# Second layer of late expert blocks: half of its row pieces as three float32r products, half as plain float32

## The reference, cut to what matters

```python
assign = jnp.argmax(x @ centroids.T, axis=1)            # one expert per token, 8 experts
xhat = (x - mu) * jax.lax.rsqrt(var + LN_EPS)           # D = 256
xn = xhat * ln_g[e] + ln_b[e]
h = relu(xn @ w1[e].T + b1[e])                          # F = 1024
y = x + h @ w2[e].T + b2[e]
out = a * y + (1 - a) * x                               # a = sigmoid(x @ centroids.T)[e]
```

## Time and profile before

| | us |
|---|---|
| median of 3 executions | 1070.82 (1069.94 to 1071.56) |
| the profiled execution, whole | 1071.78 |
| its span, first to last instruction | 1070.0 |
| PE busy in the span | 1056.2 (99%) |
| DVE / ACT / POOL busy | 798.6 / 670.3 / 495.2 |

### The profile page before, as it was taken

One profiled execution on the slowest core, in us unless ns is written; L12 is line 12 of the kernel. 1 busy time (PEld: TensorE's weight loads), 2 busy tenths in 40 slices (PEclk: granted clock), 3 DMA queues, 4 the chain that ended last, 5 costly groups with the idle time before them and its releaser, 6 DMA issues.

```text
span 1070.0 us, 24078 instructions
## 1 busy us (share of the span) xinstructions
PE 1056.2 (99%) x8454; PEld 945.2 (88%) x8454; DVE 798.6 (75%) x1907; ACT 670.3 (63%) x1820; POOL 495.2 (46%) x641
## 2 busy tenths in 40 slices
PE   8899999999999999999999999999999999999998
PEld 6789898989888888889898988888898999999997
DVE  7876888888888988888888988798886554444441
ACT  6765757575856767665757576676655646666551
POOL 2653554646464545555464646455454343222222
PEclk9999999999999999999999999999999999999999
DMA  6475676675857566767657585756467657766670
GB/s 208 99 185 135 168 188 165 168 188 141 218 137 200 150 180 157 192 165 189 169 154 196 145 219 137 199 140 156 95 162 222 250 179 267 233 225 228 226 259 30
DMA packets 159660, 190.51 MB, mean 178 GB/s; under 512 B 17453, under 2 KB 149037, under 8 KB 154672
## 3 DMA queue, kind: packets, MB, share of 16 engines
q1 hardware_dynamic: 155088, 179.09, 61.3%
q0 software_dynamic: 3360, 8.53, 2.2%
q10 hardware_dynamic: 1088, 1.31, 0.3%
HBM read 65.72 MB, written 46.07 MB: 104 GB/s over the span
## 4 chain that ended last, share of the span: by engine, by line
PE 94%; DVE 2%; POOL 1%; DMA 1%; ACT 1%; issue 1%; SPq 0%; POOLq 0%; ACTq 0%; DVEq 0%
PE psum L694 16%; PE psum L727 16%; PE psum L869 12%; PE psum L764 11%; PE psum L854 10%; PE psum L743 9%; PE psum L779 9%; PE psum L713 8%; PE psum L782 1%; POOL prob L1677 1%; DMA prob_t<-prob 1%; DVE neg_max L1291 0%; POOL w_o_lo L1731 0%; ACT prob L1037 0%; PE psum L794 0%
## 5 line engine op out<-in xcount | busy, mean ns | idle before, releaser
L1677 POOL TENSOR_TENSOR prob<-prob,inv_sum 128x512 f32<-128x512 f32 x176 | 182.8, 1053 | 203.0 <-DVE inv_sum L1297 202.3
L1037 ACT ACTIVATE prob<-psum,neg_max 128x256 f32<-128x256 f32 x352 | 164.5, 481 | 48.6 <-DVE neg_max L1291 39.6
L1291 DVE TENSOR_REDUCE neg_max<-psum 128x2 f32<-128x512 f32 x256 | 162.3, 673 | 36.5 <-PE psum L743 36.5
L869 PE MATMUL psum<-w,v_n 128*128 128x256 f32 x608 | 134.2, 379 | 0.0
L1303 DVE STREAM_TRANSPOSE prob<-prob 128x512 f32<-128x512 f32 x176 | 121.5, 699 | 9.3 <-POOL prob L1677 8.9
L869 PEld LDWEIGHTS psum<-w,v_n 128*128 128x128 f32 x608 | 114.2, 190 | 14.8
L1677 POOL TENSOR_TENSOR w_ring<-w_ring,inv_sum 128x512 f32<-128x512 f32 x76 | 78.2, 1042 | 78.4 <-DVE inv_sum L1297 78.0
L1044 ACT ACTIVATE head_out_hi<-psum 128x512 fp32r<-128x512 f32 x52 | 31.1, 598 | 114.3 <-PE psum L764 91.7
L1748 POOL DMA_INDIRECT out<-x_in,r_ring x38 | 39.8, 1048 | 127.0 <-DVE x_in L1535 126.7
L1027 ACT ACTIVATE v_n<-psum 128x512 f32<-128x512 f32 x128 | 78.3, 612 | 20.7 <-PE psum L727 20.7
L1016 ACT ACTIVATE k_hi<-psum 128x512 fp32r<-128x512 f32 x128 | 77.2, 604 | 18.1 <-PE psum L694 16.8
(11 more groups left out here) (185 smaller groups left out, 2712.6 us busy)
## 6 DMA issues: line engine op xcount, KB each, us to landing
sorted_rows<-filler SPq DMA_DIRECT2D x54, 660.0 KB, 5.0
prob_t<-prob SPq DMA_DIRECT2D x176, 128.0 KB, 2.8
w_ring<-prob SPq DMA_DIRECT2D x176, 128.0 KB
w<-in_experts SPq DMA_DIRECT2D x19, 1024.0 KB
w_ring<-in_experts SPq DMA_DIRECT2D x18, 1024.0 KB, 5.6
prob_t<-w_ring SPq DMA_DIRECT2D x76, 128.0 KB, 2.8
w_ring<-w_ring SPq DMA_DIRECT2D x76, 128.0 KB
w_ring<-normed SPq DMA_DIRECT2D x56, 128.0 KB, 3.0
```

The source lines that it names most:

```text
L869: last = pe.matmul(bank[:, 0:d_model], hid[:, s % 2, f, i * P:(i + 1) * P], w2[:, f * d_model:(f + 1) * d_model], start=(f == 0), stop=(f ...
L1037: act.activation(prob_at(u, bb)[:, :, parity, i], scores_i, ACT.Exp, bias=neg_max[:, at, i:i + 1], accum_out=prob_sum[:, at, i:i + 1]).the ...
L1291: dve.tensor_reduce(neg_max[:, (4 * u + n) % 8, :], psum[:, n, :].rearrange("p (i j) -> p i j", i=2), AXIS_X, ALU.max, negate=True).then_i ...
L1677: pool.tensor_tensor(probs, probs, inverse, ALU.mult).then_inc(s_soft, 1)
```

## The change

From block 4 on (`FIRST_SPLIT`) the second layer takes the hidden pieces 0 to 3 as high and low parts of type float32r, three products each, as the first layer does; pieces 4 to 7 stay plain. What is new per block:

- ACT (`relu_parts`): the first four activations go to a single raw buffer `hid_raw`, the last four to `hid_plain`; between the two, ACT waits for the second layer's weights and copies half of them, 128x1024, as the high part (`f_w2h`).
- DVE (`split_hidden`): for two pieces at a time a cast 128x512 to the high part and a subtraction 128x512 to the low part, behind `split_xn(s+2)` and ahead of `finish(s)`. `finish` writes its intermediate in `fin` and so waits for the buffer at its start.
- POOL (`low_weights_2`): one subtraction 128x1024 behind `add_base(s+2)` and ahead of `write_rows(s)`.
- TensorE (`layer_2_split`): waits for the four of them at its start, then 24 float32r and 8 plain matmuls.
- SP: the second-layer weights and b2 of block 5 are issued ahead of the wait for all scatters and for the late blocks' table, instead of behind the rows and first-layer weights of block 6.
- Memory: the parts lie over tensors that are dead by then (`v_n`, `prob`, `y_t`, `prob_t_even`, `head_out`, `w_o`).

```diff
+            w2_hl = [[w[:].rearrange(rule)[:, 0:FS * d_model].rearrange("p (f d) -> p f d", f=FS) for w in pair] for pair, rule in
+                     ((head_out, "p b c t -> p (b c t)"), (w_o, "p c n -> p (c n)"))]
@@ SP @@
+                load_weights_2(n_early - 1)
+                load_b2(n_early - 1)
                 scattered(n_batches)
                 run = block_steps(sp, count_empty(sp))
                 for s in range(n_early, n_slots + 1):
                     run(s, (load_vectors,), (load_rows,), (load_weights_1,))
-                    run(s - 1, (load_weights_2,), (load_b2,))
+                    if s > n_early:
+                        run(s - 1, (load_weights_2,), (load_b2,))
                     run(s, (move_rows,))
@@ PE @@
+                def layer_2_split(s):
+                    pe.wait_ge(f_w2h, s - FIRST_SPLIT + 1)
+                    pe.wait_ge(f_w2l, s - FIRST_SPLIT + 1)
+                    pe.wait_ge(f_hl, FS // 2 * (s - FIRST_SPLIT + 1))
+                    pe.wait_ge(f_ha, FC // 2 * s)
+                    def in_parts(bank, i, first):
+                        for n, (hw, hx) in enumerate(PASSES):
+                            for f in range(FS):
+                                last = pe.matmul(bank, hid_hl[hx][:, s % 2, f, i * P:(i + 1) * P], w2_hl[s % 2][hw][:, f, :],
+                                                 start=(first and n == 0 and f == 0), stop=(not first and n == 2 and f == FS - 1))
+                        return last
...
+                    bank = begin(("fy", s, 0))[:, 0:d_model]
+                    in_parts(bank, 0, True)
+                    plain(bank, 0, False).then_inc(f_y, 1)
+                    bank = begin(("fy", s, 1))[:, 0:d_model]
+                    plain(bank, 1, True)
+                    in_parts(bank, 1, False).then_inc(f_y, 1)
@@ ACT @@
+                def relu_parts(s):
...
+                    for i in range(FC // 2):
+                        act.wait_ge(f_h, FC // 2 * (s - 1) + i + 1)
+                        if i < FS // 2 and s > FIRST_SPLIT:
+                            act.wait_ge(f_hl, FS // 2 * (s - 1 - FIRST_SPLIT) + i + 1)
+                        elif i == FS // 2:
+                            wait_made(act, ("fy", s - 2, 1))
+                        for f in (2 * i, 2 * i + 1):
+                            at = slice((f % 2) * BLOCK, (f % 2 + 1) * BLOCK)
+                            dst = hid_raw[:, i, at] if f < FS else hid_plain[:, s % 2, f - FS, :]
+                            ins = act.activation(dst, psum[:, i, at], ACT.Relu, bias=b1[:, f:f + 1])
+                        ins.then_inc(f_ha, 1)
+                        if i == 1:
+                            act.wait_ge(f_w2[s % NW2], 16 * (s // NW2 + 1))
...
+                            act.activation(w2_hl[s % 2][0], w2_ring[s % NW2][:, 0:FS * d_model].rearrange("p (f d) -> p f d", f=FS),
+                                           ACT.Copy).then_inc(f_w2h, 1)
@@ DVE @@
+                def split_hidden(s):
+                    for i in range(FS // 2):
+                        dve.wait_ge(f_ha, FC // 2 * (s - 1) + i + 1)
+                        if i == 0:
+                            wait_made(dve, ("fy", s - 2, 1))
+                        hi, lo = [h[:, s % 2, 2 * i:2 * i + 2, :].rearrange("p f t -> p (f t)") for h in hid_hl]
+                        then_next(dve.tensor_copy(hi, hid_raw[:, i, :]))
+                        dve.tensor_tensor(lo, hid_raw[:, i, :], hi, ALU.subtract).then_inc(f_hl, 1)
@@ DVE, finish @@
+                        if i == 0 and s >= 2:
+                            dve.wait_ge(f_out[s % 2], 32 * (s // 2))
-                        last_reads(item, dve.tensor_tensor(upd[:, i, :], work_bank(number[item])[:, 0:d_model],
+                        last_reads(item, dve.tensor_tensor(fin[:, s % 2, i, :], work_bank(number[item])[:, 0:d_model],
                                                           b2_ring[:, s % NR, :], ALU.add))
@@ DVE @@
                 for s in range(n_early, n_slots):
                     run(s + 2, (transpose_rows,), (low_weights_1,), (split_xn,))
+                    run(s + 1, (split_hidden,))
                     run(s, (finish,))
@@ POOL @@
+                def low_weights_2(s):
+                    pool.wait_ge(f_w2h, s - FIRST_SPLIT + 1)
+                    raw = w2_ring[s % NW2][:, 0:FS * d_model].rearrange("p (f d) -> p f d", f=FS)
+                    pool.tensor_tensor(w2_hl[s % 2][1], raw, w2_hl[s % 2][0], ALU.subtract).then_inc(f_w2l, 1)
...
                         run(s + 2, (add_base,))
+                        run(s + 1, (low_weights_2,))
                         write_rows(s)
```

More of the change, by code:

```diff
@@ L35 @@
 NW, NW2, NR = 2, 3, 4
+FIRST_SPLIT = 4
 def bank_order(n_pairs, last_of_early, n_early, n_slots):
@@ L177, in build @@
             k_s = [sbuf(a, f"k_{h}", [P, 2, 2, BANK], F32R) for h in ("hi", "lo")]
+            FS = FC // 2
+            with ExitStack() as late:
+                hid_hi = sbuf(late, "hid_hi", [P, 2, FS, BLOCK], F32R)
+                sbuf(late, "hid_between", [P, 3 * FS * BLOCK])
+                hid_lo = sbuf(late, "hid_lo", [P, 2, FS, BLOCK], F32R)
             v_n = sbuf(a, "v_n", [P, 2, 2, 2, BANK])
@@ L279, in build @@
             f_ha = sem("f_ha")
+            f_hl = sem("f_hl")
+            f_w2h = sem("f_w2h")
+            f_w2l = sem("f_w2l")
             f_y = sem("f_y")
@@ L304, in build @@
             hid = v_n[:].rearrange("p s a b n -> p s (a b n)").rearrange("p s (f t) -> p s f t", f=FC)
-            flat = "p b a h i s q -> p (b a h i s q)"
-            upd = prob_t_even[:].rearrange(flat)[:, 0:2 * d_model].rearrange("p (i d) -> p i d", i=2)
+            hid_hl = (hid_hi, hid_lo)
+            hid_raw = y_t[:].rearrange("p c b t -> p c (b t)")
+            hid_plain = prob_t_even[:].rearrange("p b a h i s q -> p b (a h i s q)").rearrange("p s (f t) -> p s f t", f=FC - FS)
+            w2_hl = [[w[:].rearrange(rule)[:, 0:FS * d_model].rearrange("p (f d) -> p f d", f=FS) for w in pair] for pair, rule in
+                     ((head_out, "p b c t -> p (b c t)"), (w_o, "p c n -> p (c n)"))]
             blocks = "p (j h i s k) -> p j h i s k"
@@ L872, in layer_2, with plain @@
                         last.then_inc(f_y, 1)
+                def layer_2_split(s):
[9 more added lines that the diff above has]
+                        return last
+                    def plain(bank, i, first):
+                        for f in range(FS, FC):
+                            last = pe.matmul(bank, hid_plain[:, s % 2, f - FS, i * P:(i + 1) * P],
+                                             w2_ring[s % NW2][:, f * d_model:(f + 1) * d_model],
+                                             start=(first and f == FS), stop=(not first and f == FC - 1))
+                        return last
+                    bank = begin(("fy", s, 0))[:, 0:d_model]
[4 more added lines that the diff above has]
+                    in_parts(bank, 1, False).then_inc(f_y, 1)
                 pe.wait_ge(s_blank, 1)
@@ L950, in _ @@
                         row_transposes(s + 2)
-                    layer_2(s)
+                    if s < FIRST_SPLIT:
+                        layer_2(s)
+                    else:
+                        layer_2_split(s)
                 run = block_steps(pe, count_empty(pe))
@@ L954, in _ @@
                     run(s + 1, (layer_1,))
-                    run(s, (layer_2,))
+                    run(s, (layer_2_split,))
             @block.scalar
@@ L1139, in relu @@
                                 ins.then_inc(f_ha, 1)
+                def relu_parts(s):
+                    b1 = vec_ring[:, s % NR, 2 * KC:]
+                    if s == FIRST_SPLIT:
+                        wait_low(act, n_pairs - 1, 1)
+                    for i in range(FC // 2):
[11 more added lines that the diff above has]
+                            act.wait_ge(f_w2[s % NW2], 16 * (s // NW2 + 1))
+                            if s < FIRST_SPLIT + 2:
+                                wait_made(act, ("wout", n_batches - 1))
+                            else:
+                                wait_made(act, ("fy", s - 2, 1))
+                            act.activation(w2_hl[s % 2][0], w2_ring[s % NW2][:, 0:FS * d_model].rearrange("p (f d) -> p f d", f=FS),
+                                           ACT.Copy).then_inc(f_w2h, 1)
                 act.dma_start(c_in[:, 0:2, :], ctx_in[0:2].rearrange("b p d -> p b d")).then_inc(s_in[0], 16)
@@ L1230, in _ @@
                     high_weights_1(s + 2)
-                    relu(s + 1)
+                    relu_parts(s + 1)
                     row_gain_bias(s + 2)
@@ L1235, in _ @@
                     run(s + 2, (normalise_rows,), (high_weights_1,))
-                    run(s + 1, (relu,))
+                    run(s + 1, (relu_parts,))
                     run(s + 2, (row_gain_bias,))
@@ L1531, in finish @@
                             dve.wait_ge(f_base, s + 1)
```

(6 more changed lines are left out.)

## The result

The changed kernel takes 1080.4 us in the median of nine executions (1074.2 to 1083.2), beside 1071.0 for the kernel before: the ratio is 1.0083, with a 95% interval of 1.0066 to 1.0100. It is 0.8% slower. The forecast was 1081, in a range of 1067 to 1088. The profiled execution took 1080.92 us with a span of 1079.1; 1071.78 and 1070.0 were those of before.

A forecast was written before the change was run, and what follows sets the result against it. The bound was to pass from TensorE to the chain round SP, ACT, DVE and POOL, 27.3 us per two blocks. TensorE would end 10.1 us later, 1081.9 against the profiled 1071.78; the median lies 0.96 lower: 1081 us, range 1067 to 1088.

The forecast's parts named there:

- TensorE's saving: Second layer on TensorE: 6.33 us instead of 6.91, 0.58 less per block, 8.7 us over 15 blocks if nothing else ends last.
- The round: Chain of waits through SP, ACT, DVE and POOL, once in two blocks: 25.28 us without lock waits, 27.3 with them.
- high copy to the end of the row split, with the collision: ACT's high copy to DVE's row split: 6.98 us before, 8.04 with ACT's new copy, plus 2.0 of lock wait.
- hidden split, finish, second write: DVE's new casts and subtractions 2.35 us, finish 1.90, then 1.28 + 0.98 to the end of POOL's second write.
- from the write's end to the high copy two blocks on: Results land, SP asks for inputs, weights arrive, ACT's high copy starts: 10.73 us, the median of eleven pairs.
- The collision: POOL's new 2.30 us subtraction falls over DVE's row cast and holds it up 2.0 us per two blocks; forecast's chance 0.53.
- The row split of blocks 8 and 18: Times at which DVE's row split was to end for these blocks: 918.7 and 1056.8 us.
- Writes held up too: Rival: DVE's low copy of weights also delays POOL's second write by 2.0 us in half of five rounds: 1086 us, chance 0.15.
- the extra 1.6 for the last landing: Added at the end of the chain, since the last write-to-high-copy time was 12.36 us against the median 10.73.
- No collision: Rival: same chain without POOL and DVE holding each other up, 25.28 us per two blocks: 1069 us, chance 0.18.
- TensorE keeps its saving: Rival: the chain needs no more than TensorE's 24.16 us per two blocks, so all 15 blocks save 0.58: 1062 us, chance 0.08.
- The moved DMAs: SP issuing block 5's second-layer weights and b2 earlier pushes nothing; perhaps 0.2 us sooner for block 6, left out of the sum.

The follow-up runs named there:

- TensorE's part alone: Changed kernel with the same TensorE matmuls, but low parts left out and most new work on ACT, DVE and POOL cut to 128x8 pieces: 1068.0 us.
- ACT's copy late: Changed kernel with ACT's 128x1024 copy of second-layer weights moved from the middle of the activations to behind gain and bias: 1078.7 us.

## Why the prediction was right, step by step

- **TensorE's saving.** 6.33 us per layer, and 5.76 for a first layer that follows at once: right. It was never collected, as forecast.
- **The round.** From block 8's high copy to block 18's are 137.3 us, 27.5 per round of two blocks. By parts, the means of the five rounds of even blocks beside the terms of the sum:

| part of the round | forecast | measured |
|---|---|---|
| high copy to the end of the row split, with the collision | 8.04 + 2.0 | 9.12 = 8.01 + 1.11 held up |
| hidden split, finish, second write | 6.51 | 7.65 = 6.15 + 0.40 held up on DVE + 1.10 on POOL's write |
| from the write's end to the high copy two blocks on | 10.73 | 10.7 |
| sum | 27.3 | 27.5 |

- **The collision** is there, and was sized 0.5 us too high: DVE was held up 1.5 us per round on this chain (1.11 + 0.40 in the table), not 2.0, and it fell on the hidden split and finish too, not on the row cast alone. What fills the gap is the hold-up the other way round, of POOL's writes, 1.1 us per round, which the sum had at nothing. The Trainium skill (SBUF — State Buffer, "SBUF: two separate sides") has VectorE and GpSimd exclude each other for a whole instruction; the trace agrees, with the cast that ended 0.28 us behind POOL's subtraction.
- **The row split of blocks 8 and 18** ended at 916.4 and 1055.1; 918.7 and 1056.8 were forecast. TensorE ended at 1073.9, not 1075.2. The forecast of block 8 is off by the collision: its cast took 0.43 us, since POOL's subtraction began only at 918.32, behind the row split. The 2.3 us of head start that this gave shrank to 1.7 by block 18.
- **Writes held up too** was a rival with its own time, 1086. It happened as the rival had it: three of the five rounds, 5.5 us in all, where it had 2.5 rounds and 5.
- **That the total fits is in part luck.** From block 8's row split to block 18's 138.1 us were forecast and 138.7 measured. The held-up writes added 5.5. Against them DVE's hold-ups were 8.2 us instead of 10.0, hidden split and finish took 1.8 less than their rows (6.15 a round, not 6.51), and the extra 1.6 for the last landing did not come (10.8 us there instead of 12.36). The chain that was named is right; of the sizes of its terms, several are off and make up for each other.
- **No collision: 1069.** The kernel with POOL's subtraction cut gave 1071.1 in the median; in the profiled execution, 1065.4, it had 25.2 us per round against 25.28.
- **TensorE keeps its saving: 1062.** The condition was a round under 24.16 us. This was the incomplete part: it named one loop and there are two. With the first cut to what TensorE needs, the second, from the landing of results over SP's request and the weights' transfers back to the next landing, kept TensorE's part alone at 1068. Neither the forecast nor its range hung on it, since it only shows once the first loop is shorter than 12.9 us per block.
- **The moved DMAs**: nothing, as forecast.

## What to carry to other kernels

Before giving the bound engine less to do, walk each loop of waits that runs through the other engines once, add its instructions and landings, and compare the sum with what the bound engine will need; here a loop with some 3 us to spare in two blocks took in 3.4 us of new work (1.06 on ACT, 2.35 on DVE) and 2.6 of lock, while TensorE was to need 1.2 less. Where two engines exclude each other, reordering one of them moves the collision; what helps is to put new work where its engine waits anyway, and to ask for inputs ahead of waits that they don't depend on. And read the last iteration by itself: twice an order that shortened the loop lost more in the tail.

## What the runs showed of the hardware beyond that

- **Small result writes wait for large loads in flight.** In TensorE's part alone SP could ask 2.2 us after the write's end with 64 KB of second-layer weights behind the first-layer ones, and 4.5 to 6.7 us with 1 MB, at a DMA share of 0.7 to 1.0 until then. The size alone doesn't do it: the kernel before has the same 1 MB and 2.2 to 3.4 us, with a write that ends 10.4 us behind SP's previous request (936.67 and 947.04) where it was 7.3 (937.64 and 944.95).
- **Not every DVE instruction is held up.** The first addition of finish, which reads PSUM, took its usual 0.41 us at 918.81, inside POOL's subtraction (918.32 to 921.15); the multiply-add right behind it, which reads SBUF alone, took 2.11 us instead of 0.48.
- **TensorE's clock fell after stops.** Full speed is a granted clock of 1.00. After the stop of 3.2 us before 945.03 the first layer took 8.59 us instead of 5.76, the first 5 us of it at half of full speed, 1.2 GHz; after the one of 2.7 us before 974.71 it took 7.48. The other six stops, of 0.4 to 2.0 us, left the clock at 1.00. Stretches of the changed kernel, columns as above:

```profile
945.00:950.00 5.00, 4.97 (x23) 5.00 (x24) 4.43 (x10) 2.87 (x3) 1.02 (x1) 0.50 0.96 391
...
975.00:982.00 7.00, 7.00 (x48) 7.00 (x48) 6.26 (x9) 4.49 (x8) 3.22 (x2) 0.77 0.78 292
954.00:961.00 7.00, 7.00 (x48) 6.58 (x48) 5.29 (x8) 1.71 (x5) 4.34 (x3) 1.00 0.27 59
```

  Together some 4.5 us of slower matmuls. They aren't the cause of the loss: the kernel with ACT's copy late has a mean clock of 0.998 and the same time, so in the loop such a piece is hidden in what would else be waiting. In a tail it isn't, as the 2.90 and 4.62 us pieces show.
- **A stop costs a little of its own.** A first layer that follows a stop takes 5.98 us at full clock, one that follows at once 5.76. In TensorE's part alone one took 5.99 behind a stop of 0.04 us (940.88).
